# The opening of a cross-attention, MLA and expert kernel in another order, and a finer wait for the next block's keys

## The reference

```python
x = x + xattn(layernorm(x), ctx)      # 16 heads of 32, keys and values from 4096 context rows
x = x + mla(layernorm(x))             # latent attention, 16 heads, causal
x = x + moe(layernorm(x))             # 48 experts kept, top 8

# cross-attention, to which the change belongs
q = hs @ Wq.T + bq                    # hs: 256 x 512
k = at @ Wk.T + bk;  v = at @ Wv.T + bv   # at: 4096 x 512
scores = einsum(q, k) / sqrt(32)      # clipped, masked
ctx = softmax(scores) @ v
delta = layernorm(rs * (ctx @ Wo.T + bo)) * gamma + beta
```

## Time and profile before

| | us |
|---|---|
| median of 3 runs | 749.24 (747.83 to 749.28) |
| the profiled execution | 750.56 |
| its span in the trace | 748.7 |
| TensorE busy | 719.0 (96%) |
| VectorE busy | 610.7 (82%) |
| ScalarE busy | 428.7 (57%) |
| granted TensorE clock, mean | 0.995 |

### The profile page before, as it was taken

One profiled execution on the slowest core, in us unless ns is written; L12 is line 12 of the kernel. 1 busy time (PEld: TensorE's weight loads), 2 busy tenths in 40 slices (PEclk: granted clock), 3 DMA queues, 4 the chain that ended last, 5 costly groups with the idle time before them and its releaser, 6 DMA issues.

```text
span 748.7 us, 16362 instructions
## 1 busy us (share of the span) xinstructions
PE 719.0 (96%) x6667; PEld 446.3 (60%) x6667; DVE 610.7 (82%) x940; ACT 428.7 (57%) x585; POOL 10.3 (1%) x30
## 2 busy tenths in 40 slices
PE   7999999999999999897999988999999999999997
PEld 3644444444444444455777757677777777777774
DVE  4578999999999988687788965788888888888885
ACT  3677777777777786623568733444444444444441
POOL 2000000000000000010000000000000000000000
PEclk9999999999999999999999999999999999999999
DMA  8920101010100100031242500497777777777760
GB/s 318 330 67 1 58 2 57 3 58 7 52 3 1 43 17 2 3 133 82 75 135 87 193 36 1 137 285 236 241 223 236 239 232 244 218 241 237 243 208 29
DMA packets 29576, 93.78 MB, mean 125 GB/s; under 512 B 5920, under 2 KB 15056, under 8 KB 28112
## 3 DMA queue, kind: packets, MB, share of 16 engines
q1 hardware_dynamic: 29232, 92.97, 37.8%
q10 hardware_dynamic: 288, 0.02, 0.0%
HBM read 92.37 MB, written 0.57 MB: 124 GB/s over the span
## 4 chain that ended last, share of the span: by engine, by line
PE 85%; DVE 6%; issue 4%; ACT 3%; POOL 1%; POOLq 0%; DVEq 0%; ACTq 0%
PE pS L1134 39%; PE pP L1134 26%; PE pO L1134 10%; PE pD L1134 8%; DVE x_sb L827 2%; ACT arena L508 2%; PE pO L1462 1%; DVE arena L714 0%; DVE bn L863 0%; DVE arena L842 0%; DVE arena L962 0%; DVE arena L914 0%; DVE xn L708 0%; ACT arena L558 0%; DVE work L868 0%
## 5 line engine op out<-in xcount | busy, mean ns | idle before, releaser
L1134 PE MATMUL pS<-arena 128*128 128x256 f16 (+2 forms) x2128 | 252.6, 275 | 5.1 <-DVE arena L962 1.3
L1134 PE MATMUL pP<-arena 128*128 128x512 f16 x968 | 236.4, 383 | 7.0 <-DVE arena L714 7.0
L1134 PEld LDWEIGHTS pS<-arena 128*128 128x128 f16 (+2 forms) x2128 | 212.0, 101 | 50.0 <-ACT arena L575 2.2
L1134 PEld LDWEIGHTS pP<-arena 128*128 128x128 f16 x968 | 90.9, 99 | 131.6 <-issue 11.7
L508 ACT ACTIVATE arena<-pS,mblk 128x1024 f32<-128x1024 f32 x128 | 147.3, 1205 | 11.5 <-PE pS L1134 11.5
L962 DVE SCALAR_TENSOR_TENSOR arena<-arena 128x1536 f16<-128x1536 f32 x72 | 126.0, 1752 | 0.6 <-ACT arena L613 0.5
L651 ACT ACTIVATE arena<-pS 128x256 f32<-128x256 f32 x72 | 27.6, 383 | 155.9 <-PE pS L1134 155.9
L815 DVE TENSOR_SCALAR arena<-arena 128x1024 f32<-128x1024 f32 x128 | 87.2, 690 | 26.2 <-ACT arena L508 23.1
L613 ACT ACTIVATE arena<-arena 128x1536 f16<-128x1536 f32 x72 | 106.3, 1477 | 1.0 <-DMA arena<-in_units 1.0
L1134 PE MATMUL pO<-arena 128*32 128x256 f32 (+6 forms) x1358 | 104.4, 359 | 2.4 <-DVE arena L952 1.9
L1134 PE MATMUL pD<-arena 128*128 128x512 f16 x288 | 76.5, 379 | 1.0 <-DVE arena L1106 1.0
(11 more groups left out here) (242 smaller groups left out, 504.7 us busy)
## 6 DMA issues: line engine op xcount, KB each, us to landing
arena<-in_units SPq DMA_DIRECT2D x72, 768.0 KB, 4.7
arena<-w_scratch SPq DMA_DIRECT2D x136, 64.0 KB, 2.7
arena<-in_ctxT SPq DMA_DIRECT2D x7, 1024.0 KB, 5.1
mw_in<-in_mla_in SPq DMA_DIRECT2D x8, 832.0 KB, 6.7
mw_out<-in_mla_out SPq DMA_DIRECT2D x8, 512.0 KB, 3.7
wlatT<-in_wlatT SPq DMA_DIRECT2D x1, 1280.0 KB, 11.4
arena<-in_wkT SPq DMA_DIRECT2D x4, 256.0 KB, 4.4
arena<-in_ctxT SPq DMA_DIRECT2D x4, 256.0 KB, 6.3
```

The lines of the kernel that those rows point to most:

```text
L1134: return pe.matmul(o, lhsT, rhs, start=start, stop=stop, **kw)
```

## The change

SP's queue keeps the key weights and everything behind them; the four context chunks of block 0 are issued by ScalarE, on its queue, and the small loads follow after the splits. TensorE works each chunk in three rounds over the four key groups, high x high first, each round behind a wait for what it needs. The transposes stand behind all four chunks. The q projection is made of fp16 pairs: `wqh`, `wql` lie in `probs`, `xqh`, `xql` in `xT`; ScalarE makes high parts of q weights and x (the latter from PSUM, in place of `transposed`), VectorE the low ones. ScalarE now splits value weights before it evacuates keys, and the scale of q's evacuation is 1/256, since its operands carry 64 and 256. VectorE makes the norm before biases and mask, and the split of block 0's keys behind that of the value weights. In `project` the wait of step 0 is now one for each chunk.

```diff
@@ SP
             for c in range(HC):
                 sp.dma_start(wk32[:, c], a["wkT"][:, c]).then_inc(first_in[c], 16)
-                sp.dma_start(cbuf[:, 0, c], a["ctxT"][0][:, c]).then_inc(first_in[c], 16)
@@ ScalarE
-            for dst, src in ((xb[:, :, :], a["xb"]), (mask_i[:, :], a["mask"])):
-                act.dma_start(dst, src).then_inc(s["small_in"], 16)
+            for c in range(HC):
+                act.dma_start(cbuf[:, 0, c], a["ctxT"][0][:, c]).then_inc(first_in[c], 16)
...
-            transposed(1)
+            for dst, src in ((xb[:, :, :], a["xb"]), (mask_i[:, :], a["mask"])):
+                act.dma_start(dst, src).then_inc(s["small_in"], 16)
+            act.wait_ge(s["wq_in"], 16)
+            for c in range(HC):
+                act.activation(wqh[:, c], wqT[:, c], ACT.Copy, scale=SW).then_inc(s["wq_hi"], 1)
+            act.wait_ge(s["tr_done"], 1)
+            for i in range(2):
+                act.activation(xqh[:, 2 * i:2 * i + 2, :], pS[:, i, :].rearrange("p (c t) -> p c t", c=2), ACT.Copy,
+                               scale=SA).then_inc(s["xq_hi"], 1)
+            act.nop().then_inc(s["xT_ready"], 1)
+            act.wait_ge(s["wv_in"], 16)
+            for c in range(HC):
+                act.activation(wv16[:, 0, c], wv32[:, c], ACT.Copy, scale=SW).then_inc(s["wk_hi"], 1)
             act.wait_ge(s["prep_ready"], 1)
             for n in range(HC):
                 evac(0, 0, n)
-            act.wait_ge(s["wv_in"], 16)
-            for c in range(HC):
-                act.activation(wv16[:, 0, c], wv32[:, c], ACT.Copy, scale=SW).then_inc(s["wk_hi"], 1)
@@ VectorE
+            dve.wait_ge(s["x_in"], 16)
+            norm(x_sb, xn, 1).then_inc(s["xn_ready"], 1)
             dve.wait_ge(s["small_in"], 16 * 2)
...
-            dve.wait_ge(s["x_in"], 16)
-            norm(x_sb, xn, 1).then_inc(s["xn_ready"], 1)
-            for n in range(HC):
-                split_k(0, 0, n)
+            for c in range(HC):
+                dve.wait_ge(s["wq_hi"], c + 1)
+                dve.scalar_tensor_tensor(wql[:, c], wqT[:, c], SW, wqh[:, c], ALU.mult, ALU.subtract).then_inc(s["wq_lo"], 1)
+            for i in range(2):
+                dve.wait_ge(s["xq_hi"], i + 1)
+                dve.scalar_tensor_tensor(xql[:, 2 * i:2 * i + 2, :], pS[:, i, :].rearrange("p (c t) -> p c t", c=2), SA,
+                                         xqh[:, 2 * i:2 * i + 2, :], ALU.mult, ALU.subtract).then_inc(s["xq_lo"], 1)
             for c in range(HC):
                 dve.wait_ge(s["wk_hi"], HC + c + 1)
                 dve.scalar_tensor_tensor(wv16[:, 1, c], wv32[:, c], SW, wv16[:, 0, c], ALU.mult, ALU.subtract)\
                    .then_inc(s["wk_lo"], 1)
+            for n in range(HC):
+                split_k(0, 0, n)
@@ TensorE
             def project(b, p, n):
 
-                if n == 0:
-                    pe.wait_ge(s["ctx_lo"], 4 * (b + 1))
                 pe.wait_ge(s["proj_evac"], 8 * b + n)
                 for c in range(HC):
+                    if n == 0:
+                        pe.wait_ge(s["ctx_lo"], 4 * b + c + 1)
                     unit_part(pP[:, :], p, n, c)
...
+                for k in range(3):
+                    if k == 0:
+                        pe.wait_ge(s["ctx_hi"], c + 1)
+                    elif k == 1:
+                        pe.wait_ge(s["wk_lo"], c + 1)
+                    else:
+                        pe.wait_ge(s["ctx_lo"], c + 1)
+                    for n in range(HC):
+                        unit_part(unit_bank(0, n), 0, n, c, (k,))
+            pe.wait_ge(s["const_ready"], 1)
+            transpose_rows(1)
+            for k, (w, x) in enumerate(((wqh, xqh), (wql, xqh), (wqh, xql))):
+                for g in range(HC):
+                    for c in range(HC):
+                        if k == 0:
+                            pe.wait_ge(s["wq_hi"], c + 1)
+                            pe.wait_ge(s["xq_hi"], c // 2 + 1)
+                        elif k == 1:
+                            pe.wait_ge(s["wq_lo"], c + 1)
+                        else:
+                            pe.wait_ge(s["xq_lo"], c // 2 + 1)
+                        last = mm(pS[:, 2 + g // 2, 256 * (g % 2):256 * (g % 2) + 256], w[:, c, 128 * g:128 * g + 128],
+                                  x[:, c, :], c == 0 and k == 0 and g % 2 == 0, c == HC - 1 and k == 2 and g % 2 == 1,
+                                  skip_group_check=True)
```

More of the change, by code:

```diff
@@ L147, in build @@
         wqT = v_sb[:, 1]
+        xqh, xql = (xT[:, 2 * i:2 * i + 2, :].rearrange("p c q -> p (c q)").bitcast(f16).rearrange("p (c q) -> p c q", c=HC)
+                    for i in range(2))
         probs = take(CT * 4 * T).rearrange("p (b j q) -> p b j q", b=CT, j=4)
+        wqh, wql = (probs[:, 2 + i].rearrange("p j q -> p (j q)").bitcast(f16).rearrange("p (c n) -> p c n", c=HC)
+                    for i in range(2))
         psum4 = take(4 * T).rearrange("p (j q) -> p j q", j=4)
@@ L240, in build @@
             aux_in var_ready rstd_ready xn_ready tr_done xT_ready
-            zero_ready const_ready zc_ready prep_ready wk_hi wk_lo q_mm q_f q_hi q_lo
+            zero_ready const_ready zc_ready prep_ready wk_hi wk_lo wq_hi wq_lo xq_hi xq_lo q_mm q_f q_hi q_lo
             ctx_hi ctx_lo proj_done proj_evac k_lo
@@ L471, in _ @@
                 last = act.activation(q_f32(probs, g), pS[:, 2 + g // 2, 256 * (g % 2):256 * (g % 2) + 256],
-                                      ACT.Identity, bias=xb[:, 0, g:g + 1], scale=SA)
+                                      ACT.Identity, bias=xb[:, 0, g:g + 1], scale=1.0 / SW)
             last.then_inc(s["q_f"], 1)
@@ L1148, in transpose_rows, with unit_part @@
                 last.then_inc(s["tr_done"], 1)
-            def unit_part(bank, p, n, c):
+            def unit_part(bank, p, n, c, products=(0, 1, 2)):
                 for k, (wi, ci) in enumerate(((0, chi), (1, chi), (0, clo))):
+                    if k not in products:
+                        continue
                     start, stop = c == 0 and k == 0, c == HC - 1 and k == 2
@@ L1158, in unit_part @@
                         last = mm(bank, ci[:, p, c, 128 * r:128 * r + 128], wv16[:, wi, c, :], start, stop)
-                if c == HC - 1:
+                if c == HC - 1 and 2 in products:
                     last.then_inc(s["proj_done"], 1)
             def project(b, p, n):
-                if n == 0:
-                    pe.wait_ge(s["ctx_lo"], 4 * (b + 1))
                 pe.wait_ge(s["proj_evac"], 8 * b + n)
                 for c in range(HC):
+                    if n == 0:
+                        pe.wait_ge(s["ctx_lo"], 4 * b + c + 1)
                     unit_part(pP[:, :], p, n, c)
```

## The result

| | before | changed |
|---|---|---|
| median of 4 runs, us | 749.26 (747.83 to 749.96) | 742.95 (741.49 to 744.19) |
| ratio, 95% interval | 1 | 0.9917 (0.9892 to 0.9943) |
| the profiled execution | 750.56 | 744.19 |
| its span | 748.7 | 742.2 |

The change makes the kernel 6.3 us faster. TensorE's busy time in the changed kernel, from the page, against the earlier trace rows: the work fell by 1.6 us, the idle time from 29.7 to 24.8 us.

What follows compares the result with a forecast made beforehand. TensorE, busy 719.0 of 748.7 us, was taken as the bound. Blocks 4.4 + opening 2.9 = 7.3 us: profiled 750.56 to 743.3, median 741.9; own range 740.8 to 742.8, with the first rival 740.3 to 744.8.

Steps and rivals of the forecast that it cites:

- the blocks: Start of each key block: splitting the wait for four low chunks removes 0.74 us of TensorE idle six times, 4.4 us.
- the opening: From the start to the first scores: fp16 q projection and reordering let q end at 24.7 against 27.58, 2.9 us gained.
- the first rival: Opening pays less, by late small vectors or pairs or partly bare weight loads: gain 4.4 + 0 to 2, 742.8 to 744.8; chance 0.16.
- The slack of VectorE: In the blocks: VectorE's step takes 4.28 us against TensorE's 4.47, about 1.5 us of slack in a block.
- Rival 3: Block wait moves instead of going, VectorE being nearly full: 2.9 us from the opening alone, 746.3; chance 0.07.
- The opening up to the transposes: High products first and norm ahead of preparation: transposes at 17.4, where both meet, against 18.10; 0.7 us gained.
- The second queue: Chunk loads in the opening: valued at nothing, since transfer rate, not issuing, set landing; -1.0 us kept for the range.
- From the transposes to the scores: q in fp16 products takes 5.0 us and ends at 24.7 against 27.58; scores due at 35.1.
- At 3.7 us they are there at 16.3: Opening: small vectors issued at about 12.2 and 12.6 land at 16.3, and may come 2 us later at no cost.
- The waits on each q product: In the q projection: cost taken as 0; other bound every weight load bare, 4.8 us.
- Rivals 2 and 4: q weight loads all bare, 746.7, chance 0.04; context chunks starve on their queue, 750.8, chance 0.03.

Runs made afterwards that it cites:

- e_blocks: The kernel before with only the wait of `project` changed to one for each chunk; median 743.4 us, ratio 0.993.
- e_opening: The changed kernel with the single wait of `project` put back; median 748.58 us, ratio 0.9991.
- e_prep_late: The changed kernel with VectorE's preparation of biases and mask moved behind the low parts of q weights and x; profiled 740.36 us.
- e_small_early: The changed kernel with ScalarE issuing biases and mask directly behind the four context chunks, ahead of its splits; median 742.27 us, ratio 0.9909.
- e_backlog: The changed kernel with SP's load of block 1's context held back until biases and mask are prepared; profiled 742.02 us.
- e_few_waits: e_small_early without the waits on the second to fourth group of each set of q products; profiled 742.2 us.
- e_one_queue: The changed kernel with all bulk loads on SP's queue and the small loads first on ScalarE's; profiled 742.1 us.
- e_best: The changed kernel with e_one_queue's loads, few q waits, earlier norm statistics, transposes ahead of the last three products; median 741.09 us, ratio 0.9898.
- e_group_order: e_small_early with three products for each group behind both low parts, the order of the kernel before; profiled 744.37 us.
- e_group_again: The kernel of e_group_order run once more, unchanged; profiled 742.68 us.

## Why the prediction was right

The sum was 7.3 us, the runs gave 6.3, and the two terms missed in opposite directions: the blocks gave 4.85 for 4.4, the opening 37.94 - 36.51 = 1.43 for 2.9. The mechanism of the blocks was right. Of the opening half came, and that the median still fell inside the stated range is owed to the first rival, which the range took in, and by luck to the 0.45 us more of the blocks.

- *The blocks, 4.4 us.* Right in kind, 0.45 too small: 258.98 - 254.13 = 4.85, or 0.81 for each of six. The wait of 0.74 us is counted from the modelled end of the product before; in an unbroken stream the next starts 0.07 us ahead of that end, as after 72.56 + 1.07 = 73.63 above. The slack of VectorE was there: every kernel with the new wait has the same 254.13 us to 0.01, whatever its opening. Rival 3 falls by e_blocks.
- *The opening up to the transposes, 0.7 us.* 0.6 in the profiled pair, 17.50 for 17.4, with two misses that cancel: the last pair came 0.24 us later than before (11.21 for 10.97), the rest 0.14 us faster than forecast. The norm ahead of the preparation is what does it: from the start of the last pair's split to the transposes 7.13 us in both kernels with the old opening (before, e_blocks), 6.29 in the changed one, e_opening and e_prep_late. The prediction had chunk 2 at TensorE at 9.60; it came at 6.44 on ScalarE, and TensorE was through at about 16.6, so that the norm alone set 17.50, not both. The second queue had brought the second pair forward, which the prediction put at nothing; here it gained nothing, for the norm came later anyway.
- *From the transposes to the scores.* Here a step failed: "At 3.7 us they are there at 16.3". The 3.7 was read where the DMA engines had hardly begun (issued at 1.25) and carried over to 11.6, where 3 MB (q and value weights, next context) were still to come. It was 7.8 us. The prediction allowed 2 us of lateness; 3.1 came, 19.4 for 16.3, and the low q weights behind it cost 0.92 us (e_small_early, e_prep_late, e_backlog). The waits on each q product were taken at 0 and cost 0.24 (e_few_waits). Together with 0.1 at the transposes that makes 1.26 of the 1.41 us between the forecast 35.1 and the measured 36.51, both in the chain; the remaining 0.15 are not traced. What came is the first rival: its 742.8 to 744.8 holds the measured 742.95, which lies 0.15 above the range given for the forecast alone.
- *The second queue, valued at nothing.* Right for the last pair (e_one_queue). What the same change did to the small loads, issued late behind the chunks, it left out; with one queue and the small loads first the scores come at 34.64.
- *Rivals 2 and 4.* All weight loads bare would have made 5.2 + 4.8 = 10 us; the 48 products took 5.9 in e_small_early. No chunk starved: the last pair was split from 11.21.

The Trainium skill (DMA: Bandwidth & Descriptors, Issuing engines are not separate DMA queues) says that starting DMAs from several engines saves only the issuing time. The bulk loads agree: last pair at 10.0 to 11.0 with one queue, 10.3 to 11.3 with two. The rule of the Trainium skill cited in the prediction, that each DMA engine takes turns between its queues, packet by packet, agrees with the chunks and with the small loads: 169 and 159 packets of the two queues in the same 3 us. The prediction applied it to the chunks alone. For the small loads it means many turns, one for each row, each behind a bulk packet.

## What to carry to other kernels

A load's time to landing holds for the traffic that was queued when it was issued: before moving a small load to where large ones are in flight, look at what is queued there, at the number of its rows, and at what its first reader holds up in its engine's queue. Issuing it earlier is not free either, if the engine that issues it has other work to start. A single wait for several parts of an input, of which only the last is late, is worth splitting wherever the engine has work for the earlier parts: here it gave three quarters of the gain for three added waits. To read parts of a change below the noise of the median, compare stretches of the trace between fixed events rather than whole times.

## What the hardware showed that was not expected

- TensorE's granted clock falls to the lower level in none, one or two short spells late in the program, differently in each execution of one kernel, and the time goes with it. In one set of executions of the kernel before: 747.26 to 747.70 us in three at a mean of 1.0, 748.49 in one at 0.997, 748.67 to 750.25 in nine at 0.995. e_best: 739.6 and 739.93 at 1.0, 741.68 to 742.2 in three at 0.995, 740.49 in one at 0.996. The spells lie between 300 and 460 us, in the latent attention; the stretches of the changed kernel's profiled run, of which the third number from the end is the granted clock, show two before 400:

```profile
300.00:345.00 45.00, 41.51 (x367) 22.79 (x368) 34.90 (x78) 17.59 (x31) 4.10 (x6) 0.97 0.23 90
345.00:400.00 55.00, 52.02 (x481) 41.33 (x480) 43.49 (x84) 35.30 (x76) 0.00 (x0) 0.96 0.29 98
400.00:460.00 60.00, 55.45 (x444) 40.28 (x443) 46.01 (x102) 33.81 (x76) 1.35 (x2) 1.00 0.21 74
```

  In e_prep_late, at 1.00 throughout, the whole took 740.36 us. With two levels, 2.4 and 1.2 GHz, a mean of 0.96 is 8% of the stretch at the lower one.
- The first products of e_group_order's first chunk ran at 0.43 us for 512 columns, 1.2 GHz, while the granted clock of their stretch reads 1.00 (six products in 2 us instead of eleven in e_group_again):

```profile
8.00:10.00 2.00, 2.00 (x6) 0.67 (x5) 0.87 (x3) 0.91 (x2) 0.00 (x0) 1.00 1.06 394
```

```profile
8.00:10.00 2.00, 2.00 (x11) 0.94 (x10) 0.76 (x3) 0.82 (x2) 0.00 (x0) 1.00 1.06 401
```

  This is the rate at which every kernel here starts. The weights of the zero products are loaded every 0.43 us from the first on; in the changed kernel:

```profile
3.50 0.15 PEld L1146 LDWEIGHTS pS<-zero 128*128 128x128 f16 x1 [0.28 <-issue]
3.92 0.15 PEld L1146 LDWEIGHTS pS<-zero 128*128 128x128 f16 x1 [0.27 <-issue]
```

  The traces' records of the clock begin only when the rate rises: the first one is at 4.1 us in the changed kernel, at 10.8 in e_group_order, at 5.7 in e_group_again, at 7.1 in e_best (whose first products also took 0.4 us each), between 4.1 and 5.9 in the others. Ahead of it the views show 1.00 without a record. So at the start of a program the duration of a product has to be read, not the granted clock. TensorE had been idle for 1.72 us in both e_group_order and e_group_again, and for 1.77 in the kernel before; why the rise came so late in one execution is open.
- The time at which the same loads of an unchanged opening landed differed by 0.94 us between two executions (before and e_blocks).
